# A fused attention and feed-forward layer in fp32, one core: the last tiles' low halves, one copy and two rows of logits change their places

## What is computed

```
x = x + xattn(layernorm(x), ctx)     # 8 heads of 128, softmax over 77 keys, times Wo, plus bo
xf = layernorm(x)
out_shared = square(relu(xf @ Ws1)) @ Ws2
logits     = xf @ Wr                 # 8 experts
rw         = softmax(top2(logits))   # two weights that sum to 1
prob       = trunc(onehot(top2) * rw)   # 0 unless one weight rounds to 1
out        = x + out_shared + sum over e of prob_e * square(relu(xf @ W1_e)) @ W2_e
```

## Time and profile before

| what | value |
|---|---|
| time, median of 3 runs (range) | 117.61 us (117.22 to 117.66) |
| the profiled execution: its time, its span | 117.36 us, 115.5 us |
| busy share of the span, PE / DVE / ACT / POOL | 95% / 76% / 74% / 57% |
| granted TensorE clock, mean | 0.993 |
| start of attention of tile 14 on PE | 102.65 us |
| last output DMA issued (SP) | 111.92 us |
| flag written (DVE) | 113.74 to 113.88 us |

### The profile page before, as it was taken

The page is one execution under the profiler, slowest core; times in us unless marked ns, Lnnn a source line. Parts: engine busy times, 40 slices in busy tenths (PEclk is TensorE's granted clock), DMA queues, the critical chain, the costliest instruction groups (busy, mean ns, idle before and its releaser), DMA issues.

```text
span 115.5 us, 3118 instructions
## 1 busy us (share of the span) xinstructions
PE 109.2 (95%) x854; PEld 105.9 (92%) x854; DVE 87.8 (76%) x350; ACT 85.5 (74%) x348; POOL 65.5 (57%) x106
## 2 busy tenths in 40 slices
PE   6976999999999999999999999999999999989981
PEld 6974999899998989999999999999999999979970
DVE  1009888569889697797979797797979696798963
ACT  4006925997948979898988889898988889994320
POOL 2005735855372965785676578657746865469250
PEclk9999999999999999999999999999999999999997
DMA  3799999994000200040005001300500050031032
GB/s 63 252 336 357 354 355 350 346 349 160 6 6 0 91 0 3 6 146 35 0 0 182 0 0 61 121 0 0 182 0 0 0 182 3 0 124 57 38 136 98
DMA packets 11815, 12.70 MB, mean 110 GB/s; under 512 B 1056, under 2 KB 10272, under 8 KB 11808
## 3 DMA queue, kind: packets, MB, share of 16 engines
q1 hardware_dynamic: 11520, 12.36, 32.4%
q10 hardware_dynamic: 288, 0.26, 0.7%
HBM read 8.42 MB, written 2.10 MB: 91 GB/s over the span
## 4 chain that ended last, share of the span: by engine, by line
PE 80%; DVE 7%; DMA 4%; ACT 2%; SPq 2%; issue 2%; POOL 1%; DVEq 0%; ACTq 0%
PE o_ps L435 8%; PE o_ps L437 8%; PE o_ps L436 8%; PE s_ps L435 7%; PE s_ps L437 7%; PE s_ps L436 7%; PE g_ps L493 6%; PE f_ps L523 4%; DMA wqt_sb<-in_wq_t 4%; PE g_ps L506 3%; PE f_ps L435 2%; PE g_ps L449 2%; ACT probs L712 1%; PE f_ps L437 1%; PE f_ps L436 1%
## 5 line engine op out<-in xcount | busy, mean ns | idle before, releaser
L712 ACT ACTIVATE probs<-s_ps,neg_max,rstd 128x77 f32<-128x77 f32 x112 | 45.2, 425 | 4.0 <-DVE neg_max L950 4.0
L840 POOL TENSOR_TENSOR probs<-probs,recip 128x308 f32<-128x308 f32 x27 | 18.9, 701 | 23.4 <-DVE recip L956 23.3
L712 ACT ACTIVATION_READ_ACCUMULATOR probs<-s_ps,neg_max,rstd 128x1 f32 x112 | 24.0, 214 | 0.0
L435 PE MATMUL o_ps<-u_hi,pt_hi 128*128 128x256 f32 (+1 forms) x80 | 22.7, 284 | 0.5 <-DVE pt_lo L964 0.5
L437 PE MATMUL o_ps<-u_lo,pt_hi 128*128 128x256 f32 (+1 forms) x80 | 22.4, 280 | 0.0
L436 PE MATMUL o_ps<-u_hi,pt_lo 128*128 128x256 f32 (+1 forms) x80 | 22.4, 280 | 0.0
L435 PE MATMUL s_ps<-a_hi,xt_hi 128*128 128x308 f32 x64 | 22.1, 345 | 0.0
L437 PE MATMUL s_ps<-a_lo,xt_hi 128*128 128x308 f32 x64 | 19.5, 304 | 0.0
L436 PE MATMUL s_ps<-a_hi,xt_lo 128*128 128x308 f32 x64 | 19.4, 303 | 0.0
L435 PEld LDWEIGHTS o_ps<-u_hi,pt_hi 128*128 128x128 f32 (+1 forms) x80 | 15.0, 188 | 0.9 <-DVE pt_lo L964 0.9
L436 PEld LDWEIGHTS o_ps<-u_hi,pt_lo 128*128 128x128 f32 (+1 forms) x80 | 15.1, 188 | 0.0
(11 more groups left out here) (188 smaller groups left out, 270.6 us busy)
## 6 DMA issues: line engine op xcount, KB each, us to landing
xt_sb<-in_x_t SPq DMA_DIRECT2D x8, 256.0 KB, 6.4
x_sb<-in_x SPq DMA_DIRECT2D x8, 256.0 KB, 6.3
x_sb<-x_tr SPq DMA_DIRECT2D x7, 256.0 KB, 2.3
out<-y_sb SPq DMA_DIRECT2D x6, 256.0 KB, 2.3
wqt_sb<-in_wq_t SPq DMA_DIRECT2D x4, 256.0 KB, 5.2
wo_sb<-in_wo SPq DMA_DIRECT2D x1, 1024.0 KB, 8.9
wk_sb<-in_wk_p SPq DMA_DIRECT2D x3, 256.0 KB, 3.2
wv_sb<-in_wv_p SPq DMA_DIRECT2D x2, 384.0 KB, 6.2
```

The source lines that it names most:

```text
L435: pe.matmul(out_ap, hi, rhs_hi, start=first, stop=False)
L712: e = act.activation(probs_of(t)[:, par, h * TK:(h + 1) * TK], s_ps[:, 2 * par + half, (h - half * H // 2) * TK:(h - half * H // 2 + 1) * TK],
L840: pool.tensor_tensor(rows, rows, recip[:, par, hs].unsqueeze(2).broadcast_to([P, H // 2, TK]), ALU.mult).then_inc(probs_ready, 1)
```

## The change

DVE: `step(13)` ends after the gap of tile 12. The low half of tile 14's first pair comes next, then the reciprocals of tile 15, then the second pair. The output rows of tile 11 move behind the low half of the last chunk and tile 15's first partial reciprocals, to where DVE copied the turned rows of x1 of tile 13. ACT makes that copy instead, behind its exponentials of tile 15, when DVE has read the last of tile 14 from the same bank (`ptlo_last`). PE's wait for this copy moves from before the first turned chunk of tile 15 to before its fifth, which is the one that writes to that bank. The logits of tile 15 go to the bank of `f_ps`, those of 14 stay in bank 1 of `s_ps`, and DVE waits for each by itself.

```
-        late_logit_bank = s_ps[:, 1, :]
+        late_logits_of = {LAST - 1: s_ps[:, 1, 0:E], LAST: s_ps[:, 1, E:2 * E], LAST + 1: f_ps[:, 0:E]}
...
# PE, in transposes(t, par)
+                        if isinstance(t, int) and t == TILES - 1 and c == KC - 1:
+                            pe.wait_ge(g_ready, LAST)
...
# PE, between attention(LAST, 0) and transposes(LAST + 1, 1)
-            pe.wait_ge(g_ready, LAST)
...
# ACT, between exps(LAST + 1, 1, 1) and copy_pairs(LAST + 1, 1)
+            act.wait_ge(ptlo_last, LAST + 1)
+            copy_x1(LAST, g_sb)
...
# DVE, in top_logits
-                    dve.wait_ge(last_logits, 1 if t < LAST else 3)
-                    rows = late_logit_rows(t)
+                    dve.wait_ge(last_logits, t - LAST + 2)
+                    rows = late_logits_of[t]
...
# DVE, in step, behind logit_gap(t - 1, 1 - par)
+                if last_one:
+                    return
                 if live(t - 2, TILES):
                     result(t - 2, par)
                 reciprocals(t + 2, par, 0)
...
# DVE, behind the loops
-            lo_of_transposes(LAST, 0)
+            lo_of_pair(LAST, 0, 0)
+            reciprocals(LAST + 1, 1, 0)
+            lo_of_pair(LAST, 0, 1)
             dve.wait_ge(g_done, LAST + 1)
             dve.tensor_copy(pt_hi[:, PB:PB + 2 * P], g_ps[:, LO:LO + 2 * P]).then_inc(pthi_last, 1)
             lo_of_last(LAST, 0)
             part_reciprocals(H // 2, exp_part, 1)
-            dve.tensor_copy(g_sb[:, :], g_ps[:, XO:XO + D]).then_inc(g_ready, 1)
+            result(LAST - 3, 1)
             part_reciprocals(H - 2, exp_done, 2 * TILES)
```

More of the change, by code:

```diff
@@ L298, in h2_of @@
             return h2_end[:, :] if isinstance(t, int) and t == TILES - 1 else h2[:, par, :]
-        def late_logit_rows(t):
-            return late_logit_bank[:, (t - LAST + 1) * E:(t - LAST + 2) * E]
         x_rows = x.rearrange("b (n p) d -> p n b d", p=P)
@@ L616, in late_logits @@
                 for c in range(DCH):
-                    mm = pe.matmul(late_logit_rows(t), x1_t[:, c * P:(c + 1) * P], wsr_c[:, c, FE:NL],
+                    mm = pe.matmul(late_logits_of[t], x1_t[:, c * P:(c + 1) * P], wsr_c[:, c, FE:NL],
                                    start=c == 0, stop=c == DCH - 1)
@@ L956, in reciprocals, with lo_of_pair @@
                 dve.reciprocal(recip[:, par, hs], sums[:, par, hs]).then_inc(recip_ready, 1)
+            def lo_of_pair(t, par, pair):
+                at = slice(2 * pair * P, 2 * (pair + 1) * P)
+                dve.wait_ge(pthi_ready, pt_count(t, pair))
+                dve.tensor_tensor(pt_lo[:, at], (g_ps[:, 0:2 * P], s_ps[:, 2 * par, 0:2 * P])[pair], pt_hi[:, at].bitcast(F32),
+                                  ALU.subtract).then_inc(ptlo_ready, 1)
             def lo_of_transposes(t, par):
                 if late(t):
[L961 to L965, removed]
+                    lo_of_pair(t, par, 0)
+                    lo_of_pair(t, par, 1)
                     return
@@ L1187, in _ @@
             for t in (LAST, LAST + 1):
-                dve.tensor_copy(logits[:, t, :], late_logit_rows(t)).then_inc(logits_done, 1)
+                dve.tensor_copy(logits[:, t, :], late_logits_of[t]).then_inc(logits_done, 1)
             dve.wait_ge(gs, GATE_STEPS - 1)
```

## The result

| | before | changed |
|---|---|---|
| time, median of 14 runs each | 117.10 us | 116.32 us |
| profiled execution: its time, its span | 117.36, 115.5 us | 116.54, 114.7 us |
| attention of tile 14 starts (PE), after tile 13's | 3.36 us | 3.09 us |
| attention of tile 15 starts (PE), after tile 13's | 6.55 us | 6.28 us |
| first MAX of the end (DVE), after tile 13's | 12.90 us | 12.31 us |

What follows compares the result with a forecast made beforehand. PE was taken to be busy for 95% of the span, so only the stretch behind the loops mattered, where its chain leaves PE for DVE. Forecast: 117.46 - 0.35 (0.27 and 0.08) = 117.1 us, range 116.4 to 117.6.

Steps and rivals of the forecast that it cites:

- First term: At tile 14, DVE's first low half goes ahead of output rows and reciprocals: attention earlier, 0.27 us (bounds 0.26 and 0.30).
- forecast from L1171: At tile 15, DVE's L1150 is held under POOL's L903 until 0.14 us ahead of L903's end, 104.08 to 104.27.
- The copy on ACT at nothing: Behind ACT's exponentials: the 0.38 us copy costs nothing, as 0.5 us of idle ACT covers it.
- Second term: At the end, first MAX 0.39 us earlier, but `gap_var` held 0.31 us by POOL's power: 0.08 us gained.
- the sign of being wrong that the prediction named: At the end, `gap_var` keeps its 0.22 us (then 116.8), or tile 15's fourth chunk starts later than 104.8.
- the bounds: For the logits at the end: 0.39 us gained if POOL's power holds nothing, 0.08 if it holds `gap_var`.
- The base: Whole kernel: starting time of the forecast, 117.46 us, the mean of four times of the kernel before.
- The power holds nothing: At the end, POOL's power doesn't delay `gap_var`: the whole 0.39 us come through, 0.66 in all, 116.8 us; chance 0.35.
- Tile 15 gave nothing back: Rival at tile 15: L1150 gets ahead of L903, delays the third chunk and returns the first term; 117.3 us, chance 0.12.
- The slower one: At tile 15, L1150 is held through POOL's 2.40 us power, fourth chunk 2.2 us later; 119.6 us, chance 0.08.

Runs made afterwards that it cites:

- e5_dve_copy: The changed kernel, but DVE copies x1's turned rows of tile 13 as before and ACT doesn't; 116.30 us, ratio 0.9932.
- e4_power: The changed kernel with an added, unused power of 128x8 on spare SBUF rows ahead of POOL's last power; median 116.32 us, ratio 0.9942.
- e2_banks: The kernel before with tile 15's logits in a bank of their own, nothing else; 116.73 us, ratio 0.9959.
- e6_act_copy: The changed kernel with DVE's old order at tile 14 (output rows and reciprocals ahead of the first low half); 116.60 us, ratio 0.9962.

## Why the prediction was wrong, step by step

- **First term, 0.27 us: the mechanism right, the exact size in part luck.** 0.27 at tile 14 and 0.27 at tile 15 in the trace, 0.26 alone. I had 0.30 at tile 14 and took 0.03 off at tile 15. The first low half did start 0.30 us sooner, but it took 0.42 us instead of 0.39, so PE got 0.27; and tile 15 took nothing off. Two errors of 0.03 cancel. Of the details at tile 15 two were off. In the kernel before POOL's L903 was not queue-bound: in the changed one it came 0.04 us nearer to the start of tile 13's attention instead of 0.10 us later, because before it had waited for the partial reciprocals, not for the POOL instruction ahead of it. So PE's third chunk didn't wait, and the fourth only 0.04 us. And the multiply of heads 6 and 7 was held 0.08 us (0.40 instead of 0.32), not 0.19; it was let go near 103.93, 0.15 us ahead of L903's end, as forecast from L1171.
- **The copy on ACT at nothing: right.** It ran at 103.39 and 0.66 us of idle time were left; put back on DVE, it costs 0.04 us at the flag.
- **Second term, 0.08 us: this step failed.** It gave 0.40. MAX came earlier by what I said; `gap_var` met the power as I said, 0.45 us ahead of its end; but the power did not hold it (0.22 us, not 0.53), the sign of being wrong that the prediction named. I took the price from L896, an add that streams 256 columns, as the nearest row for a power of four columns. The experiments set the two apart in one place of one program: an add of 1.04 us on 512 columns holds, powers of 1.02 and 1.65 us on 4 and 8 columns don't. The rule that I weighed, in the Trainium skill ("SBUF — State Buffer", section "Who interferes with whom"), is that a VectorE instruction with two SBUF inputs contends with a GpSimd instruction that reads SBUF, under an exclusive lock. The adds and multiplies here agree with it up to their last 0.14 to 0.21 us. The powers, which read SBUF too, don't once they are 0.15 us under way, and there the measurement decides. The rows of before already held a hint that I had passed over: L1150 lies beside the power of 12 columns for 0.26 of its 0.32 us; it had started first, so it proved nothing about a power that is under way, but an estimate midway between the bounds would have been fairer than the upper one.
- **The base, 117.46 us: 0.36 too high.** It was the mean of four executions; 14 runs have a median of 117.10. With it and the two terms as measured, 117.10 - 0.27 - 0.40 = 116.43, against 116.32 measured; the 0.11 us left are less than the medians of the changed kernel differ from sitting to sitting. Base and second term together put the time under the range: with either of them right, 116.75 or 116.79, it would have lain inside.
- **The rivals.** "The power holds nothing" came true in its mechanism, for a DVE instruction that starts inside the power, and in its 0.66 us (0.67 in the traces). Tile 15 gave nothing back. The slower one, heads 6 and 7 behind the power of 2.40 us, didn't happen, and e5_dve_copy shows why: there the multiply starts inside that power and isn't held.

## What to carry to other kernels

Whether a neighbour on POOL blocked a DVE instruction was here a question of what that POOL instruction did, or on how many columns, and not only of where its operands lay: look for a row of the same operation and size, and if there is none, keep both bounds at like weight. For an end that is a chain of short dependent steps on one engine, split the waits so that each part starts with its own input, and interleave independent steps; an old wait further on (0.18 us here) is a cushion that hides delays up to its size. Effects smaller than the scatter of whole times are read in a trace as distances from a fixed instruction behind the noisy start.

## What the runs showed that was not expected

- **A power on POOL that is under way didn't hold a DVE instruction with two SBUF inputs.** Five multiplies of one column shown here inside powers (the changed kernel, its two banks alone, two in e4_power, one behind the add) took 0.22 us, one of 154 columns 0.32. Each started 0.15 us or more into the power.
- **At a power's start the two do meet, and there the power waits.** The power of 12 columns took 2.29 us in e5_dve_copy, where the multiply of 154 columns came after its start. In the other eleven traces that multiply was already running, and the power took 2.35 to 2.40 us: it ended 2.135 to 2.139 us behind the multiply's end in each of them. The powers of 4 and 8 columns took 1.02 and 1.65 us, so 2.29 for 12 is the next of equal steps, and what is above it is waiting. So the power does want something that the multiply holds, but only near its start; that this is the reading of its few columns fits and isn't measured.
- **The start scatters more than the change is worth.** Tile 13's attention began between 98.69 and 99.58 us in three traces of the same changed kernel; the distance from there to tile 14's attention was 3.09 us in all three. Medians of that kernel in three sittings, not all on one chip, were 116.32, 116.16 and 116.63 us.
- **One or two tiles in most traces run faster.** The 15 matmuls of a tile's attention follow one another at 118 ns, but at 113.8 in tile 15 (before), in the tile at 78.31 us (changed), in tile 14 (e2_banks and e6_act_copy): 0.06 us in the tile. Ten of the twelve traces have one or two such tiles, in places that differ and in part recur. The granted clock was 1.00 in tile 15 (before) and in the tile at 78.31 us (changed), as in the slower tile at 73 us of both. The cause is open.
